# Gate and up quantised apart from down; denser slots for the last FFN of batches 13 and 14; the last reciprocals picked into the scores' banks

## What is computed

```
x = x + 0.5 * ffn(layernorm(x), w_gate, w_up, w_down)      # first layer
x = x + attn(layernorm(x), w_q, w_k, w_v, w_proj, ...)      # 16 heads of 64, softmax, layernorm, gamma, beta
x = x + 0.5 * ffn(layernorm(x), w_gate, w_up, w_down)      # last layer
ffn(x) = q(silu(q(x) q(w_gate)^T) * (q(x) q(w_up)^T)) q(w_down)^T      # 352 hidden
q(t): blocks of 16 along the last axis, scale = max|block| / 6, rounded to the FP4 grid, times scale
```

## Time and profile before

| | us |
|---|---|
| runs, without the profiler | 2203.10, 2203.17, 2203.94 |
| median | 2203.17 |
| profiled execution, its own time | 2205.3 |
| span of its instructions | 2203.5 |
| PE busy in the span | 2099.7 (95%) |
| DVE, POOL, ACT busy | 1627.1, 1429.2, 1161.3 |

### The profile page before, as it was taken

One profiled execution on the slowest core, in us unless ns is written; L12 is line 12 of the kernel. 1 busy time (PEld: TensorE's weight loads), 2 busy tenths in 40 slices (PEclk: granted clock), 3 DMA queues, 4 the chain that ended last, 5 costly groups with the idle time before them and its releaser, 6 DMA issues.

```text
span 2203.5 us, 39642 instructions
## 1 busy us (share of the span) xinstructions
PE 2099.7 (95%) x15051; PEld 1164.6 (53%) x15051; DVE 1627.1 (74%) x2633; ACT 1161.3 (53%) x1766; POOL 1429.2 (65%) x1287
## 2 busy tenths in 40 slices
PE   3899999999999999999999999999999999999984
PEld 2455555555555555555555555565555555555543
DVE  5575778778687877878777787877868787776645
ACT  2455555646546555555556555564655646465432
POOL 3375676757577675766767576675757767585643
PEclk8899999999999999999999999999999999999996
DMA  2000000000000000000000000000000000000000
GB/s 61 1 7 2 7 2 2 7 7 7 7 7 7 3 7 7 7 7 2 12 2 7 7 7 7 2 7 7 7 7 6 7 2 7 7 3 7 2 7 10
DMA packets 165786, 15.89 MB, mean 7 GB/s; under 512 B 146592, under 2 KB 165216, under 8 KB 165600
## 3 DMA queue, kind: packets, MB, share of 16 engines
q1 hardware_dynamic: 165600, 13.36, 5.2%
HBM read 7.03 MB, written 4.19 MB: 5 GB/s over the span
## 4 chain that ended last, share of the span: by engine, by line
PE 85%; DVE 9%; issue 3%; POOL 1%; ACT 1%; DMA 0%; SPq 0%; POOLq 0%
PE pS L1042 23%; PE pO L1070 19%; PE pX L1054 6%; PE pX L1094 5%; PE pM L1199 5%; PE pO L1026 5%; PE pM L1026 4%; PE pM L1082 3%; DVE nmax L871 3%; PE FpF L379 2%; PE LpF L379 2%; PE FpF L342 2%; PE LpF L355 2%; PE LpF L342 2%; PE FpF L355 1%
## 5 line engine op out<-in xcount | busy, mean ns | idle before, releaser
L739 POOL TENSOR_TENSOR ES<-ES,E 128x512 f32<-128x512 f32 x512 | 676.7, 1343 | 284.1 <-ACT E L818 280.0
L818 ACT ACTIVATE E<-pS 128x1024 f32<-128x1024 f32 x512 | 524.4, 1024 | 512.8 <-PE pS L1042 505.3
L871 DVE TENSOR_REDUCE nmax<-pX 128x2 fp32r<-128x1024 f32 x512 | 621.8, 1214 | 189.6 <-PE pX L1054 185.8
L1070 PE MATMUL pO<-E,VA 128*64 128x512 f32 x2048 | 524.1, 611 | 2.0 <-DVE KL L989 1.8
L733 POOL TENSOR_TENSOR ES<-E 128x512 f32<-128x512 f32 x256 | 323.0, 1283 | 174.9 <-ACT E L818 174.9
L1054 PE MATMUL pX<-KH,QH 64*128 64x512 f32 x1024 | 248.2, 425 | 11.4 <-DVE nmax L871 8.0
L1042 PE MATMUL pS<-QH,KH 64*128 64x512 f32 x1024 | 255.3, 495 | 0.5 <-ACT E L818 0.5
L1042 PEld LDWEIGHTS pS<-QH,KH 64*128 64x128 f32 x1024 | 95.4, 183 | 235.6 <-issue 230.1
L1054 PEld LDWEIGHTS pX<-KH,QH 64*128 64x128 f32 x1024 | 187.2, 306 | 49.4 <-DVE nmax L871 24.1
L1070 PEld LDWEIGHTS pO<-E,VA 128*64 128x64 f32 x2048 | 114.9, 135 | 168.8 <-issue 168.8
L1042 PE MATMUL pS<-SH,onesr 64*128 64x512 f32 x1024 | 203.4, 393 | 0.0
(11 more groups left out here) (241 smaller groups left out, 3684.6 us busy)
## 6 DMA issues: line engine op xcount, KB each, us to landing
RROW<-RC SPq DMA_DIRECT2D x504, 2.0 KB, 2.0
xin<-in_L_attn_x SPq DMA_DIRECT2D x16, 256.0 KB, 2.8
SH<-nmax SPq DMA_DIRECT2D x256, 2.0 KB, 2.0
LC<-LROW SPq DMA_DIRECT2D x252, 2.0 KB, 2.1
out<-X SPq DMA_DIRECT2D x15, 256.0 KB, 2.5
E<-in_L_attn_w_q SPq DMA_DIRECT2D x1, 512.0 KB, 4.3
E<-in_L_attn_w_k SPq DMA_DIRECT2D x1, 512.0 KB, 5.5
wv<-in_L_attn_w_v SPq DMA_DIRECT2D x1, 512.0 KB, 6.6
```

The source lines that it names most:

```text
L739: ins = g.tensor_tensor(ES[i % 3][:, hd, :], ES[i % 3][:, hd, :], E[s][:, hd, :], ALU.add)
L818: a.activation(E[s][:, :, :], pS[:, :, :], ACT.Exp).then_inc(s_exp, 1)
L871: v.tensor_reduce(nmax[px % 2][:, :, t:t + 1], pX[:, :, :], AX.X, ALU.max, negate=True).then_inc(s_max, 1)
L1070: ins = pe_.matmul(pO[half(hd), :], VA[of][:, kt, j * 128 + 64 * hd:j * 128 + 64 * hd + 64], E[kt][:, hd, :], start=kt == 0, stop=kt == KT ...
```

## The change

1. The start: gate and up are quantised first, as 768 columns, with a semaphore of their own for their DMAs; then x; then down's 384 columns. Down's transposes stand on PE at slot 4 of the head, its copy to wdT on ACT at slot 5, and the first down waits for it.
2. Batch 13 gets a table of its own, `ThirdLayer`: up in slots 33 to 36, both halves quantised at once, down in slot 45 and not 57.
3. Batch 14 (`LateLayer`) has gate in slots 26 and 27, up in 28 and 29, quantisation in 29 to 31, turn_h in 31 and 32, down in 34, add in 37. It uses two banks, LpF and FpF, in turn; `paired` sets its waits.
4. The reciprocals of the last two pairs are picked at step 3 of the loop's pair 128 into the two banks of pS, before the projection, where before they went to pM and pO one step later.
5. The count of output DMAs is kept in two semaphores by the parity of the batch.

```diff
@@ class LastLayer:
-    lead, batches = -1, range(0, B - 2)
+    lead, batches = -1, range(0, B - 3)
@@ class HeadLayer(FirstLayer):
+    turn_w = 4
+class ThirdLayer(LastLayer):
+    batches = range(B - 3, B - 2)
+    up = (33, 34, 35, 36)
+    max_h, divide_h, magic_h, round_h, rescale_h = (35, 37), (36, 38), (36, 38), (37, 39), (38, 40)
+    turn_h, down, add = (39, 40, 42, 43), (45,), (46,)
@@ class LateLayer(LastLayer):
-    up = (33, 34, 35, 36)
-    max_h, divide_h, magic_h, round_h, rescale_h = (36, 37), (36, 37), (37, 38), (38, 39), (39, 40)
-    turn_h, down, add = (40, 41, 42, 43), (44,), (45,)
+    mom_x, scale_x, apply_x = 20, 20, 21
+    max_x, divide_x, magic_x, round_x, rescale_x, turn_x = 22, 22, 22, 23, 24, 25
+    gate, up = (26, 26, 27, 27), (28, 28, 29, 29)
+    max_h, divide_h, magic_h, round_h, rescale_h = (29, 30), (29, 30), (29, 30), (30, 31), (30, 31)
+    turn_h, down, add = (31, 31, 32, 32), (34,), (37,)
@@ bank
+        if self.paired(c) and k % 2 == 1:
+            return self.other
@@ pe_up
+        elif self.paired(c):
+            pe.wait_ge(self.s_silu, 4 * c + min(k + 3, 4))
+            wait(pe, self.s_h, 4 * c + k - 1 if k > 1 else 0)
@@ pool, the start
-                L.qh.divide(nc, pool, 0, L.h[:, 0:NW], slice(0, NW // BLK))
+                L.qh.divide(nc, pool, 0, L.h[:, GATE_UP], WB[0])
                 F.pool_divide_x(pool, 0)
-                L.qh.rescale(nc, pool, 0, L.h[:, 0:NW], slice(0, NW // BLK))
+                L.qh.rescale(nc, pool, 0, L.h[:, GATE_UP], WB[0])
                 F.pool_rescale_x(pool, 0)
+                L.qh.divide(nc, pool, 1, L.h[:, DOWN], WB[1])
+                L.qh.rescale(nc, pool, 1, L.h[:, DOWN], WB[1])
@@ vector, the start
-                dve.wait_ge(s_wraw, 96)
-                L.qh.maxima(nc, dve, 0, L.h[:, 0:NW], slice(0, NW // BLK))
+                dve.wait_ge(s_wraw, 64)
+                L.qh.maxima(nc, dve, 0, L.h[:, GATE_UP], WB[0])
@@ vector, i == NP + 1 and s == 0
                             dve.wait_ge(s_rb, NP - 1)
-                            v.tensor_tensor(OT[(NP - 2) % 3][:, :], OT[(NP - 2) % 3][:, :], pM[:, :], ALU.mult)
-                            v.tensor_tensor(OT[(NP - 1) % 3][:, :], OT[(NP - 1) % 3][:, :], pO[:, :], ALU.mult).then_inc(s_norm, 1)
+                            dve.wait_ge(s_ot, NP)
+                            for j in range(2):
+                                last = OT[(NP - 2 + j) % 3]
+                                ins = v.tensor_tensor(last[:, :], last[:, :], pS[:, j, :], ALU.mult)
+                            ins.then_inc(s_norm, 1)
@@ tensor
-                        if i == NP + 1 and s == 0:
-                            pe.wait_ge(s_pick, 4)
-                            pe.wait_ge(s_inv, 1)
-                            pe.wait_ge(s_norm, NP - 2)
-                            pe.wait_ge(s_ot, NP)
-                            pe_.matmul(pM[:, :], pick[:, 0, :], LROW[:, :], start=True, stop=True)
-                            pe_.matmul(pO[:, :], pick[:, 1, :], LROW[:, :], start=True, stop=True).then_inc(s_rb, 1)
+                        if i == NP and s == 3:
+                            pe.wait_ge(s_pick, 4)
+                            pe.wait_ge(s_inv, 1)
+                            pe.wait_ge(s_exp, 4 * NP)
+                            for j in range(2):
+                                ins = pe_.matmul(pS[:, j, :], pick[:, j, :], LROW[:, :], start=True, stop=True)
+                            ins.then_inc(s_rb, 1)
```

More of the change, by code:

```diff
@@ L288, in apart, with paired @@
         return c == self.alone
+    def paired(self, c):
+        return self.other is not None and c == self.alone - 1
     def bank(self, c, k):
+        if self.paired(c) and k % 2 == 1:
+            return self.other
         return self.spare[k] if self.apart(c) else self.pF
@@ L338, in pe_gate @@
             pe.wait_ge(self.s_xqT, c + 1)
+        elif self.paired(c):
+            wait(pe, self.s_silu, 4 * c + k - 1 if k > 1 else 0)
         elif not self.apart(c):
@@ L364, in pe_h @@
             pe.wait_ge(self.s_h, 4 * c + 4)
+        elif self.paired(c):
+            wait(pe, self.s_hT, 4 * c + k - 1 if k > 1 else 0)
         elif not self.apart(c):
@@ L468, in make_program @@
     NW = FT * FP
+    GATE_UP = slice(0, 2 * FP)
+    DOWN = slice(2 * FP, NW)
+    WB = [slice(w.start // BLK, w.stop // BLK) for w in (GATE_UP, DOWN)]
     def steps(eng, body):
@@ L537, in make_program @@
         F.lone = L.lone = pX[:, 1, :]
+        F.other, L.other = None, F.pF
         norm_x = Norm(m, "nx", 1e-5)
@@ L565, in make_program @@
         s_res = m.sem("s_res")
-        s_out = m.sem("s_out")
+        s_out = [m.sem(f"s_out{k}") for k in range(2)]
         s_side = m.sem("s_side")
@@ L644, in _ @@
                 steps(sp, body)
-                sp.wait_ge(s_out, 16 * (B + 1))
+                sp.wait_ge(s_out[0], 16 * (B // 2))
+                sp.wait_ge(s_out[1], 16 * (B // 2 + 1))
             @block.gpsimd
@@ L745, in _ @@
                 norm_x.apply(nc, act, 0, F.xn, xin)
-                L.qh.magics(nc, act, 0, L.mag[:, 0:NW], L.h[:, 0:NW])
+                L.qh.magics(nc, act, 0, L.mag[:, GATE_UP], L.h[:, GATE_UP])
                 F.act_magic_x(act, 0)
-                for k in range(3):
+                for k in range(2):
                     act.wait_ge(s_wT_ps, k + 1)
-                    src = (pO, pM, pX[:, 0, :])[k]
-                    dst = wguT[:, k, :] if k < 2 else wdT[:, :, :].rearrange("p t d -> p (t d)")
-                    a.activation(dst, src[:, 0:FP], ACT.Copy, scale=1.0 if k < 2 else 0.5).then_inc(s_wT, 1)
+                    a.activation(wguT[:, k, :], (pO, pM)[k][:, 0:FP], ACT.Copy).then_inc(s_wT, 1)
+                L.qh.magics(nc, act, 1, L.mag[:, DOWN], L.h[:, DOWN])
                 def first_ffn_psum(b, t, plan):
+                    if plan is HeadLayer and batch_at(plan, plan.turn_w + 1, b, t):
+                        act.wait_ge(s_wT_ps, 3)
+                        a.activation(wdT[:, :, :].rearrange("p t d -> p (t d)"), pX[:, 0, 0:FP], ACT.Copy,
+                                     scale=0.5).then_inc(s_wT, 1)
                     for c in batch_at(plan, plan.turn_x + 1, b, t):
@@ L1118, in first_ffn @@
                         F.pe_up(pe, c, k)
+                    if plan is HeadLayer and batch_at(plan, plan.turn_w, b, t):
+                        pe.wait_ge(L.qh.s_quant, 2)
+                        turn_weight(2)
                     for c, k in parts_at(plan, plan.turn_h, b, t):
@@ L1121, in first_ffn @@
                     for c, k in parts_at(plan, plan.down, b, t):
+                        if c == 0 and k == 0:
+                            pe.wait_ge(s_wT, 3)
                         F.pe_down(pe, c, k)
```

39 lines of the change are left out of this document (26 added, 13 removed).

## The result

The changed kernel takes 2207.85 us at the median (2204.56 to 2209.24, 20 runs), the kernel before beside it 2203.49 (2199.05 to 2207.35, 20 runs). The ratio is 1.0019, its 95% interval 1.0013 to 1.0026: 4.4 us slower, where 1.3 us less was forecast, and above the range. Both differences have to be explained, and the gap between them too.

What follows compares the result with a forecast made beforehand. PE was taken to bound the middle, and chains the two ends. On the profiled execution 2205.3 - 4.8 + 15.9 - 7.6 - 4.8 = 2204.0, 1.3 us less; on the median 2201.9, with an 8-in-10 range of 2195.2 to 2206.8.

Steps and rivals of the forecast that it cites:

- The start's term: Weight quantisation at the start: earlier maxima 1.6 plus fewer columns 3.6 minus down's magic 0.4, 4.8 us less.
- The middle: Up to 2120 us: PE-bound, so an instruction moved between slots costs there what it saves; only waits count.
- Batches 13 and 14 in the last loop: PE before the last pair's step 2: seven more gates and ups 4.1, batch 13's waits 1.2, batch 14's x 1.8 us.
- POOL, 15.6: Last pair: POOL's divides, rescales and ES take 13.0 us plus 2.6 for DVE's rounding beside them, before the row sums.
- Row sums at the low clock: Last pair's row sums on PE: twice the 1.04 us of full clock, because PE's gaps lower the clock.
- Down to ny_stats: From row sums to batch 15's start: down 4.5, copy and picks 2.4, projections 3.5, add 0.8; 11.2 us, 7.6 less.
- batch 15's chain: Last batch's chain, no longer shared with batch 14: 2.8, 1.1 and 0.9 us less, together 4.8 less.
- (a): Rival, chance 0.27: overlap works, waits vanish, DVE and POOL don't disturb each other, clock stays up; 7.7 us less, 2194.2.
- (b): Rival, chance 0.13: PE's clock is low from the row sums to the last projection; 7.1 us more, 2209.0.
- (c): Rival, chance 0.10: x's path or down's work replaces the weights' at the start; gain 1.6 not 4.8, 2205.1.
- the picks alone: End of the kernel: picking into pS alone saves nothing, since the picks still wait for the reciprocal.

Runs made afterwards that it cites:

- e2: Kernel before with changes 2, 3 and 5 (tables of batches 13 and 14, two banks), old start and picks: 2209.06 against 2204.05 us, ratio 1.0020.
- e4: Kernel before with change 4 (last reciprocals picked into pS one step earlier) and change 5: 2202.47 against 2204.05 us, ratio 0.9994.
- e5: The changed kernel run again without an edit: 2207.87 us against 2203.53 for the kernel before, ratio 1.0021.
- e1: Kernel before with change 1 (gate and up quantised ahead of down's weights) and change 5: 2201.12 against 2204.05 us, ratio 0.9991.
- e6: Changed kernel with batch 14's hidden rows quantised behind the last pair: 2197.59 us, against 2203.53 for the kernel before, ratio 0.9972.
- e10: Changed kernel with batch 13's second half and rounding one slot later: 2208.81 us against 2201.45 for the kernel before, ratio 1.0028.
- e3: Kernel before with changes 2 and 5 alone (batch 13's table, two output semaphores): 2206.49 against 2204.05 us, ratio 1.0011.
- e12: Kernel before with changed start, picks, batch 13's old slots, batch 14 later, its hidden rows behind the last pair, down in slot 41: 2187.53 against 2197.80 us.
- e8: e6 with down's magic behind the first FxqT copy and LastLayer's calls ahead of ThirdLayer's: 2196.37 us against 2203.53 for the kernel before, ratio 0.9972.

## Why the prediction was wrong, step by step

**The start's term, 4.8. This is the step that failed, and the largest miss.** Gate and up did go through the quantisation sooner, as I said, but the size was wrong. Against the execution that the sum was made on, the copy to FxqT came 3.6 us earlier; against other executions of the same old start 2.8 to 3.1. The maxima began at 5.6 to 5.9 as I said, but with all three weights they begin at 7.32 only in the profile of before, and at 6.20 to 6.54 in e2 to e4: against those the DMA is worth 0.4 to 0.9, not 1.6. From the maxima to the copy it takes 14.6 us with the old start in all four executions and 12.4 to 12.5 with the new one: 2.1 to 2.2 less, where the sum has 3.6 - 0.4 = 3.2. The rounding was scaled from a row where little of it ran beside POOL, and took 1.84 in place of the 1.09 of the sum. Down's magic ahead of the copy cost 0.6 to 0.7 and not 0.4. At the first scores four executions with the old start lie at 72.9 on average, five with the new one (after, e5, e1, e6, e10) at 71.0: 1.9 us, with a spread of 6 us in the first group. So few profiles bound this stage poorly, but e1's ratio says 2 as well, and its interval leaves out 4.8. So the other half of the term fails too, that everything up to the first scores moves along with the copy: at the copy these averages are 3.1 apart. What takes away the rest is that e3 and e4 are fast behind the copy, at a higher granted clock; none of the ten executions with the new start is. Whether that is chance or the new start's doing stays open. The other executions lean to the second: the mean granted clock over the span is 0.985 or 0.986 in 8 of the 33 executions of before beside e1, which take 2201.4 at the median where the other 25 take 2204.2, and in none of the 11 of e1. The miss explains most of why the profiled pair (+1.2) and the runs (+4.4) differ: I had corrected the level of the profiled execution by 2.1 us, but not the term, which was measured from an execution that came late. That the pair shows 4.9 at the first scores, nearly the 4.8 of the sum, is luck.

**The middle, nothing.** I named no cost there. The order of the calls cost 0.8. The other 1.3 us of the profiled pair I put down to stalls of mostly 0.65 us ahead of projections, of which after has 17 and before 14. Their number varies from one trace to another, from 5 to 17, and the length of the middle goes with it: e12 has 5 stalls and the shortest middle, after and e2 have 17 and 15 and the longest.

**Batches 13 and 14 in the last loop, 4.1 + 1.2 + 1.8 = 7.1.** Measured 8.0, in e5 9.6. The place of each wait was right. Batch 13's table costs 2.17 in e3, not 1.2; x's waits are 0.95 + 0.62 + 0.49 = 2.1, not 1.8; the last of them, PE's own for x, I had not named. What was missing is the clock: where it falls after the wait of slot 7, some 1.5 us are lost behind it. I had counted PE's clock only at the end, since the rows had it at 1.00 up to 2120.

**POOL, 15.6.** Right: 2130.78 to 2146.41. It began 2.8 us later than I put it in this pair, which is the middle's 2.1 and the last loop's 0.9. Its parts were less so: a divide took 0.65 more, an ES pair 1.3 more, and a wait of 0.83 for the rounding, where I had 0.65 four times. The four roundings beside it took 1.51, 1.96, 1.69 and 1.84 where one of 704 columns alone takes 0.89 (e8 and e10), so DVE lost 3.4 us. The Trainium skill (SBUF — State Buffer, Who interferes with whom) has a DVE instruction with two inputs in SBUF contend with a POOL instruction that reads SBUF, and calls the port that they share an exclusive lock: it is the order of issue that decides which of the two waits. The rows agree, and on both sides: each rounding issued while POOL was at work is long, and so is POOL's divide of 2.04, issued while a rounding was under way. On the path, which is POOL's, this came to 0.65 + 1.3 + 0.83 = 2.8, near the 2.6 that went by the row and not the 3.4 that went by the page. e6 shows that the term is POOL's: without these instructions ahead of the last ES the stage takes 8.96 and not 20.08.

**Row sums at the low clock, 2.08.** Measured 1.93.

**Down to ny_stats, 11.2; batch 15's chain, 4.8 less.** Measured 11.30, with parts of 4.54, 0.42, 1.91, 1.90 and 1.77, and 5.1 less. These held. That the picks alone save nothing held within what e4 can tell (0.3 to 0.5); with the tables they save 0.5 to 1.0.

**The rivals.** (a) Waits that vanish: no, all of them came. (b) The clock low through to the last projection: picks and projections ran at full clock, so it wasn't that; the median of 2207.85 lies near this rival's 2209.0 by chance. (c) A start that gives 1.6: near what it gives on average (1.9), but not for its reason: x's own path didn't take the weights' place, and down's magic in front of the copy did, but at 0.6 to 0.7 us and not 3.2. The sum with the sizes above, -1.9 + 0.8 + 8.0 to 9.6 + 8.6 to 9.1 - 7.5 - 5.2, is 2.8 to 4.9 us (-1.9 at the start, 0.8 for the order of the calls); the runs say 2.9 to 5.7. What stays open is what makes the stalls in the middle and their share, why the start is fast in some executions, and how often the clock falls in slot 7: it did in two of the six executions with that wait (after, e2, e3, e5, e6, e8), too few to weigh it.

## What to carry to other kernels

A single profile has stages that repeat to 0.1 us and others that move by several; find out which is which before a term is measured from one, and set the term against the average of the moving stage. Cut the moving stage once more to see where the executions part: here it was not at the copy alone, but at PE's work behind it. Filling idle slots with another batch's work pays on the engine that waits, and costs on the one that its result goes through: here PE's gates and ups could go ahead of the last pair, but POOL's divides and rescales had to stay behind it (10 us between e5 and e6). A class or table of its own for one batch also reorders the slots that it shares unchanged.
